# VectorE takes a second square in every eighteen steps of the rational convolution's pipeline

## What is computed

```python
def _L2_conv_ref(x, A, Bc):
    ...
    pw = wins[..., None] ** jnp.arange(DEG_P, dtype=x.dtype)
    P = jnp.einsum('pbchwi,fcpi->fpbchw', pw, A)
    Q = 1.0 + jnp.abs(jnp.einsum('pbchwi,fcpi->fpbchw', pw[..., 1:1 + DEG_Q], Bc))
    out = jnp.sum(P / Q, axis=(1, 3))
```

## Time and profile before

| | |
|---|---|
| median of 3 runs | 11572.25 us (11549.52 to 11573.89) |
| profiled execution, its own time | 11549.69 us |
| its span in the profile | 11547.8 us |
| PE busy in the span | 8600.7 us (74%) |
| DVE busy | 8534.8 us (74%) |
| ACT busy | 6994.4 us (61%) |
| POOL busy | 5920.0 us (51%) |
| third layer, first to last square | from 6001.7 to 10547.7 us |
| squares on POOL, L1232 | 2248, 4282.8 us busy |

### The profile page before, as it was taken

One profiled execution on the slowest core, in us unless ns is written; L12 is line 12 of the kernel. 1 busy time (PEld: TensorE's weight loads), 2 busy tenths in 40 slices (PEclk: granted clock), 3 DMA queues, 4 the chain that ended last, 5 costly groups with the idle time before them and its releaser, 6 DMA issues. The chain is left out here.

```text
span 11547.8 us, 174635 instructions
## 1 busy us (share of the span) xinstructions
PE 8600.7 (74%) x48250; PEld 4203.0 (36%) x48250; DVE 8534.8 (74%) x10195; ACT 6994.4 (61%) x7795; POOL 5920.0 (51%) x2841
## 2 busy tenths in 40 slices
PE   0788758884888488853018888888888888885699
PEld 0566536663666366631002222222222222221233
DVE  1787668775777478754648888888888888886677
ACT  0455435553555255533438888888888888885454
POOL 0223223221333123210039999999999999995243
PEclk9899879987999689976559999999999999997899
DMA  2000000000000100011422232223322222224444
GB/s 90 1 0 0 15 23 0 0 11 26 0 0 7 30 1 0 0 38 56 148 83 59 67 65 60 59 59 66 65 61 59 59 63 65 64 59 100 122 115 99
DMA packets 254148, 548.42 MB, mean 47 GB/s; under 512 B 38656, under 2 KB 173088, under 8 KB 239552
## 3 DMA queue, kind: packets, MB, share of 16 engines
q1 hardware_dynamic: 253366, 539.26, 19.3%
HBM read 353.17 MB, written 185.94 MB: 47 GB/s over the span
## 5 line engine op out<-in xcount | busy, mean ns | idle before, releaser
L1232 POOL TENSOR_TENSOR l_a<-l_a 128x1018 f32<-128x1018 f32 x2248 | 4282.8, 1940 | 296.4 <-ACT l_a L1398 286.6
L1360 DVE TENSOR_TENSOR l_r<-l_pps,l_a 128x509 f32<-128x509 f32 x4232 | 2641.4, 679 | 641.3 <-PE l_pps L1245 641.3
L1398 ACT ACTIVATE l_a<-l_a 128x2036 f32<-128x2036 f32 x1193 | 2268.6, 1902 | 178.0 <-DVE l_a L1366 106.4
L1391 ACT ACTIVATE l_a<-l_qps 128x1018 f32<-128x1018 f32 x1725 | 1748.1, 1020 | 531.2 <-PE l_qps L1245 494.4
L1245 PE MATMUL l_qps<-l_mv,l_wst 123*128 123x509 bf16 x4246 | 1317.1, 393 | 865.8 <-DMA l_mv<-pw 577.0
L654 POOL TENSOR_TENSOR a_pr<-a_pr 128x768 f32<-128x768 f32 x384 | 898.7, 2340 | 1639.3 <-DVE a_pr L569 1624.2
L1245 PE MATMUL l_pps<-l_mv,l_wst 123*128 123x509 bf16 x4232 | 1356.6, 389 | 145.8 <-DVE l_r L1360 137.5
L454 POOL TENSOR_TENSOR a_pr<-a_qkv 128x768 f32<-128x768 f32 x128 | 386.7, 3040 | 2065.3 <-ACT a_qkv L696 2065.3
L683 ACT ACTIVATE a_g<-a_fps 128x512 f32<-128x512 f32 x1152 | 680.6, 597 | 989.8 <-PE a_fps L436 988.4
L436 PE MATMUL a_fps<-a_hbt,a_wfc 96*128 96x512 f32 x2304 | 1217.6, 664 | 70.3 <-ACT a_g L683 70.3
L407 PEld LDWEIGHTS a_cps<-a_wfp,a_g 128*128 128x128 f32 x9216 | 1120.7, 197 | 204.6 <-issue 154.8
(11 more groups left out here) (164 smaller groups left out, 11770.4 us busy)
## 6 DMA issues: line engine op xcount, KB each, us to landing
l_mv<-pw SPq DMA_DIRECT2D x1608, 79.5 KB
l_gx<-g SPq DMA_DIRECT2D x66, 1040.0 KB
planes<-l_s SPq DMA_DIRECT2D x67, 1018.0 KB, 4.6
l_sh<-planes SPq DMA_DIRECT2D x536, 127.2 KB, 6.3
pw<-pw_hi SPq DMA_DIRECT2D x165, 127.2 KB
pw<-pw_mid SPq DMA_DIRECT2D x165, 127.2 KB
pw<-pw_lo SPq DMA_DIRECT2D x165, 127.2 KB
a_tb<-g SPq DMA_DIRECT2D x16, 1031.9 KB
```

Of the source, the lines that this page charges most:

```text
L1232: g.tensor_tensor(a, a, a, ALU.mult).then_inc(sq_p, 1)
L1360: v.tensor_tensor(to, pps[:, (2 * m + h) % P_BANKS, 0:SUB], pair_of(A, m)[:, h, :], ALU.mult).then_inc(mul_done, 1)
L1391: s_.activation(pair_of(A, s), q, ACT.Abs).then_inc(abs_a, 1)
L1398: s_.activation(a, a, ACT.Abs_reciprocal_sqrt, bias=1.0).then_inc(root_done, GROUP)
```

## The change

A second pair of each eighteen, number 14, is squared by VectorE instead of GpSimd. The sets of the absolute values are left as they are.

```diff
 CYCLE = 2 * NPAIR2
 ABS_DVE = {1, 5, 8, 12, 15}
-SQ_DVE = {3}
+SQ_DVE = {3, 14}
 LAG_ROOT, LAG_SQ, LAG_P, LAG_MUL, LAG_SUM, LAG_COPY, LAG_LATE = 1, 7, 8, 8, 10, 11, 12
```

## The result

The changed kernel takes 11732.68 us (median of 4 runs, 11719.33 to 11759.77), the kernel before 11573.07 us (4 runs): a ratio of 1.0136, 95% interval 1.0119 to 1.0152. It is slower by some 160 us, and the forecast of 11715 us lies 18 us under it.

The account below looks back on a forecast made before the run. The prediction took the ring TensorE to VectorE to TensorE as the bound, not GpSimd. 66 × (0.25 + 1.9) = 142 us plus 10 of clock gave +152, so 11702 or 11724; forecast 11715 us, range 11685 to 11775.

Parts of the forecast that it names:

- What bounds the layer: Third layer: the ring TensorE to VectorE to TensorE sets the pace, ScalarE beside it; not GpSimd, though busy for 94%.
- The signs: Profile after: 265 VectorE squares, three GpSimd squares per supertile at 2.86 us, GpSimd busy about 4099 us, supertile 71 us.
- Step 3: Just behind the gather: VectorE's new square takes 1.21 us while GpSimd idles; 0.25 us left per supertile.
- Step 21: Before that step's products: GpSimd starts 0.11 us ahead, VectorE's new square takes 2.85 us; 1.9 us left per supertile.
- the catch at step 28: VectorE's old square starts 2.2 us late but ends 1.9 late, with a GpSimd square released by ScalarE's root.
- first rival: VectorE gets there first at step 21, its square taking 1.21 us: 36 us in all, 11586 or 11608; chance 0.18.
- The clock: TensorE's granted clock sometimes falls after the new stall at step 21: between 0 and 54 us, taken as 10.
- GpSimd's loss: Each square on VectorE costs GpSimd 0.98 us too, in an engine that nobody waits for; priced at nothing.
- The sum: 66 × (0.25 + 1.9) = 142 us for the two new squares, plus 10 for the clock: +152 us.

Follow-up runs that it names:

- the two runs that give GpSimd more: Against the kernel before, VectorE squares only pair 32 of 36 (11467.83 us, ratio 0.9871) or no pair (11477.56 us, ratio 0.9883); GpSimd squares the rest.
- the run with step 21 alone: Kernel before plus only the new VectorE square at step 21 (pairs 3, 14, 21 of 36 on VectorE): 11735.81 us, ratio 1.0122.
- the run with the cleared tile: Changed kernel plus GpSimd clearing a small unread tile before its square of pair 17, once per supertile: 11671.7 us, ratio 1.0057.
- the spare square: Kernel before, GpSimd keeping all its squares, plus VectorE squaring pair 14 into an unread tile at the change's places: 11693.13 us, ratio 1.0092.
- the square behind the products: Changed kernel with VectorE's square at step 21 issued behind that step's two products, 1.2 us later: 11653.97 us, ratio 1.0039.

## Why the prediction was right

- **What bounds the layer.** Read rightly: not GpSimd. Shown by the run without pair 14's square (no gain) and by the two runs that give GpSimd more (gains). That a delay of VectorE passes on shows at step 21: the 2.00 us that are left behind step 28 in the run with step 21 alone are all still there at the next output sum.
- **The signs.** As forecast: 265 squares of VectorE, 198 of GpSimd at 2.86 us (three per supertile), GpSimd busy for 4124.7 us where 4099 and some 20 were written, and 71.5 us per supertile.
- **Step 3.** Forecast 1.21 us of square and 0.25 us left; measured 1.21 and 0.24.
- **Step 21.** Forecast that GpSimd starts 0.11 us ahead and the square takes 2.85 us; measured 0.12 and 2.85. Forecast 1.9 us left, measured 2.00: the step that was off is the catch at step 28. The old square was to end 1.9 us late after starting 2.2 late, so to take 1.4 us; it took 1.54. The root that releases GpSimd there came 2.0 us late and not 1.9. The order itself hung on a tenth of a microsecond: 0.31 us more on GpSimd turned it, in the run with the cleared tile, to that of the prediction's first rival.
- **The clock.** The smallest term of the sum, and the one most off. Two places in the trace after, each 4.5 us with the stall of step 21 and the 3.4 us behind:

```profile
8061.50:8066.00 4.50, 2.73 (x15) 0.66 (x15) 4.50 (x5) 4.50 (x4) 4.50 (x2) 1.00 0.90 145
8066.10:8069.50 3.40, 3.31 (x12) 0.68 (x13) 2.94 (x5) 0.16 (x1) 3.40 (x2) 0.50 0.06 18
8491.70:8496.20 4.50, 2.73 (x16) 0.67 (x15) 4.50 (x5) 4.50 (x4) 4.50 (x2) 1.00 0.82 151
8496.20:8499.60 3.40, 2.69 (x16) 0.73 (x16) 3.40 (x6) 1.43 (x3) 3.40 (x3) 1.00 0.16 40
```

  The same stall (2.73 us busy of 4.5) is followed by 1.2 GHz in one supertile and by 2.4 GHz in another. Over the layer the mean clock fell from 0.97 to 0.96. With 66 × (69.25 − 67.01) = 148 us accounted for, 171.5 − 148 = 23 us are left in the profiled executions for this term, where 10 were taken. The clock records of the traces bear this out. Within the layer TensorE was at half clock for 237 us before and for 337 after; half clock begins right behind the stall of step 21 in 18 supertiles after and at this place in none before. What the layers have beyond 66 times the shortest length follows this time in the other runs too: +31 us with 358 us at half clock (the spare square), +26 with 367 (the cleared tile), −42 with 108 (the square behind the products). What decides in which supertile the clock falls wasn't tried.
- **The first rival**, VectorE first at step 21, was priced too low. With that order, in the run with the cleared tile, a supertile is 1.0 us longer and not 0.55. VectorE is 0.55 us late at step 22, as forecast, but it still has 0.52 of this at step 27, where 0.3 were to be left, and step 28 adds 0.23.
- **GpSimd's loss** was costed at nothing, since no row waits for GpSimd. It does reach VectorE, without a semaphore: VectorE's square at step 28 can't end before GpSimd's current one. Counted from the output sum of the shortest supertile, that square of GpSimd ends at 46.29 us before, and at 48.54 in the change, 47.29 with the cleared tile, 47.49 with the spare square, 47.57 with the late one: 2.25, 1.00, 1.20 and 1.28 us later. The supertiles are 2.24, 1.00, 1.19 and 1.28 us longer. In the change and with the late square a root of ScalarE releases GpSimd in the steps before, as the prediction has it; in the other two GpSimd runs from step 21 to step 28 without a gap, and most of what arrives is the time for which it was blocked at step 21 (0.93 and 0.98 us).
- **The sum** of 152 us stands against 171.5 us in the layer of the profiled executions: 6 us are the catch at step 28, 13 the clock. Of the 18 us by which 11715 lies under the median, 9 come from setting the base between the lowest run and the median.

The Trainium skill's rule (SBUF — State Buffer, "Who interferes with whom") that issue order decides between a VectorE instruction with two SBUF inputs and a GpSimd one was borne out at both orders: 2.85 us for VectorE when it is 0.12 us behind, 1.21 when it is 0.14 ahead, with GpSimd paying 2.81. The advice in the Trainium skill's Perfetto Trace Analysis, "Optimizing Scalar/DVE Operations", that moving work between these engines might not help was too mild here: the move to VectorE cost 1.4%, and the move to GpSimd gained 1.2 to 1.3%.

## What to carry to other kernels

The busiest engine isn't the one to relieve if no row shows anyone waiting for it: leave its work out once (as with pair 14) before paying another engine to take it. Where two engines exclude each other, an instruction's price at a place is as a rule its length plus what is left of the other's, and that is read from the timeline to a tenth of a microsecond. An engine for which no row waits can still delay another in this way, so its delays aren't free even where its relief is. In the change the phase repeats in all 66 supertiles, so a bad one is paid in every turn, and moving one instruction by a microsecond can be worth more than moving it to another engine.

## What wasn't expected of the hardware

- The phase is kept without jitter: VectorE's square at step 21 took 2.85 us (to 0.01) in every supertile, 1.66 in the late variant and 1.21 in the one with the cleared tile. Only with the spare square did ten of 66 differ.
- A blocked VectorE instruction isn't always next: once it was passed over five times and took 11.57 us.
- Variants with the same number of instructions differ in how often TensorE is granted half its clock: for 337 us of the layer in the change, for 108 with the square 1.2 us later (a mean of 0.97 and 0.99 between 6100 and 10400). The late variant's ratio to the kernel before is 0.0097 under that of the change; by the shortest supertiles, 66 × (69.25 − 68.29) = 63 us, only 0.0055 of it is the phase of the square.
